# Second cross-attention of a two-layer decoder: three score rounds of four heads become two rounds of two heads

## The reference, cut to what matters

```
x = _layernorm(x + _L1_xattn_ref(ctx_1024, ctx_1024, x, Wv, Wk, Wq, Wo, bo))
```

## Time and profile before

| what | value |
|---|---|
| median of three runs | 2841.48 us |
| the profiled execution's own time | 2838.83 us |
| its span from first to last instruction | 2837.0 us |
| mean granted TensorE clock | 0.942 of full |
| windows of the fifth block (first to last exponential) | about 2003 to 2493 us |

### The profile page before, as it was taken

One profiled execution on the slowest core, in us unless ns is written; L12 is line 12 of the kernel. 1 busy time (PEld: TensorE's weight loads), 2 busy tenths in 40 slices (PEclk: granted clock), 3 DMA queues, 4 the chain that ended last, 5 costly groups with the idle time before them and its releaser, 6 DMA issues.

```text
span 2837.0 us, 37833 instructions
## 1 busy us (share of the span) xinstructions
PE 2598.1 (92%) x14306; PEld 1562.2 (55%) x14310; DVE 1468.7 (52%) x3205; ACT 1126.7 (40%) x1614; POOL 1035.0 (36%) x702
## 2 busy tenths in 40 slices
PE   5786999999999999996999999688999999889997
PEld 3343556555556555654565666455434444468886
DVE  3443555555555555554433333266777776355555
ACT  3544344444444444442121121133576666631111
POOL 4666366666765676562100000242121112010001
PEclk8996999999999999997899999898899999789998
DMA  2001100000000000003899999410000000000000
GB/s 103 9 9 34 36 12 16 29 19 12 27 18 19 12 12 25 12 1 125 347 389 381 365 384 385 169 32 22 15 17 17 21 17 9 13 14 23 23 23 32
DMA packets 60196, 229.01 MB, mean 81 GB/s; under 512 B 16536, under 2 KB 30512, under 8 KB 44144
## 3 DMA queue, kind: packets, MB, share of 16 engines
q1 hardware_dynamic: 54128, 209.01, 20.1%
q0 software_dynamic: 3584, 9.84, 1.2%
q10 hardware_dynamic: 2304, 7.75, 0.7%
HBM read 216.73 MB, written 9.70 MB: 80 GB/s over the span
## 4 chain that ended last, share of the span: by engine, by line
PE 75%; DVE 7%; ACT 7%; issue 4%; DMA 3%; POOL 3%; SPq 0%; POOLq 0%; ACTq 0%; DVEq 0%
PE PS L680 8%; PE PS L1475 7%; PE PS L2074 6%; PE PS L663 6%; PE PS L711 5%; PE PS L1493 4%; PE PS L721 4%; PE PS L2062 4%; ACT y_P L1192 4%; PE PS L1120 3%; PE PS L695 3%; DMA m_fb<-in_m_fb 3%; PE PS L1137 3%; PE PS L1103 2%; PE PS L744 2%
## 5 line engine op out<-in xcount | busy, mean ns | idle before, releaser
L944 POOL TENSOR_TENSOR x_A<-x_A,x_P 128x1024 f32<-128x1024 f32 x190 | 451.1, 2374 | 205.8 <-ACT x_P L791 191.8
L871 DVE CUSTOM_DVE_ANT_0 x_junk<-PS,x_mb 128x512 bf16<-128x512 f32 x512 | 331.0, 685 | 351.8 <-PE PS L695 351.6
L1243 DVE TENSOR_REDUCE y_Mx<-PS 128x1 f32<-128x512 f32 x512 | 326.2, 684 | 124.7 <-PE PS L1137 123.1
L791 ACT ACTIVATE x_P<-PS,x_kb 128x1024 f32<-128x1024 f32 x256 | 271.9, 1111 | 224.4 <-PE PS L667 222.3
L1192 ACT ACTIVATE y_P<-PS 128x1024 f32<-128x1024 f32 x256 | 248.4, 1024 | 128.7 <-PE PS L1120 127.1
L1475 PE MATMUL PS<-m_w,m_xt 128*128 128x512 f32 x624 | 283.2, 597 | 0.6 <-issue 0.6
L680 PE MATMUL PS<-x_P,x_V 128*64 128x512 f32 x1024 | 247.1, 604 | 0.0
L663 PE MATMUL PS<-x_Q,x_K 64*128 64x512 f32 x1536 | 229.8, 403 | 0.0
L2074 PE MATMUL PS<-n_xp,n_wp 128*128 128x512 f32 x816 | 211.4, 409 | 4.3 <-POOL n_wp L2190 4.3
L1696 POOL DMA_INDIRECT m_xb<-xd,m_idxi x39 | 37.0, 949 | 404.9 <-PE PS L1463 372.0
L1475 PEld LDWEIGHTS PS<-m_w,m_xt 128*128 128x128 f32 x624 | 116.5, 192 | 116.9 <-issue 115.0
(11 more groups left out here) (331 smaller groups left out, 4210.9 us busy)
## 6 DMA issues: line engine op xcount, KB each, us to landing
m_w<-in_m_w SPq DMA_DIRECT2D x39, 2048.0 KB, 11.5
m_fb<-in_m_fb SPq DMA_DIRECT2D x39, 1024.0 KB, 13.3
m_v<-in_m_w SPq DMA_DIRECT2D x39, 1024.0 KB
x_w<-in_x_w SPq DMA_DIRECT2D x32, 384.0 KB, 3.1
ys<-m_yb SPq DMA_DIRECT2D x39, 128.0 KB
n_wg<-in_n_w SPq DMA_DIRECT2D x17, 256.0 KB, 2.8
x_cT<-in_ctxT SPq DMA_DIRECT2D x4, 1024.0 KB, 5.8
y_c<-in_ctxT SPq DMA_DIRECT2D x6, 512.0 KB, 3.6
```

The costliest lines, as they stand in the source:

```text
L791: act.e.activation(Pt[gt % 6][:], PS[:, 2 * i:2 * i + 2, :], ACT.Exp, bias=kb[u // 8 % 2][:, kt:kt + 1], scale=scale).then_inc(s["exp"], 1)
L871: dve.e.tensor_tensor_reduce(junk[j % 2][:], ring.bank("max", v, j), mb[b % 2][:, half * 512:half * 512 + 512], 1.0, -3e38, ALU.add, ALU.m ...
L944: pool.e.tensor_tensor(A[u % 2][:], Pt[(gt - 1) % 6][:] if kt == 1 else A[u % 2][:], Pt[gt % 6][:], ALU.add).then_inc(s["add"], 1)
L1243: dve.e.tensor_reduce(Mx[v % 2][:, h, qt, half:half + 1], ring.bank("max", v, j), AX.X, ALU.max).then_inc(s["red"], 1)
```

## The change

- The scores are made in two halves of two heads: heads 0 and 1 ("sc", 0), then heads 2 and 3 ("sc", 1). Each half has two rounds instead of three: 8 matmuls for four heads instead of 12.
- The columns of the projection matrices are doubled, so that rows 16 to 31 of a band hold the keys and the queries a second time. The second key tile now holds the keys as they are in rows 0 to 15 and the low part in rows 16 to 31. The first round multiplies it with the doubled high part of the queries, 32 rows deep. The second round is high keys x low queries, with row 16 for the ones and the maxima, 17 rows deep.
- GpSimd makes the second key tile with two instructions (a product with the column `part`, then a subtraction) in place of one. ScalarE's high part of the keys is a copy without a bias.
- The ones of row 16 are written by one more DMA per group (4 partitions x 4 KB), ahead of the four rows of the maxima, which go to `Q[..][1]`.
- Each half waits only for the exponential that last read its two banks, and each exponential only for its half.
- The order of a window becomes: first half of the scores, two maxima (now of heads 2 and 3), the side work except pv and ev, second half, two maxima (heads 0 and 1), pv, ev, and what `after` lists. "turn" moves into `after`, "mq" behind the first two maxima.

```diff
             after = {0: [("st", -2, 0), ("xb", 0, 0)], 1: [("nr", -2, 0)], 2: [("tp", -2, 0)], 3: [("rec", -1, 0)], 4: [("tp", -2, 1)],
-                     5: [("mul", -1, 0)], 6: [("res", -1, 1)], 7: [("res", -1, 3)]}
-            at = {t: ([("mq", 1, 0)] if t == 5 else []) + maxima(t)[:2] + between[t] + maxima(t)[2:] + after[t] for t in range(T)}
+                     5: [("turn", 1, 0), ("mul", -1, 0)], 6: [("res", -1, 1)], 7: [("res", -1, 3)]}
+            at = {t: [("sc", 0, 0), *maxima(t)[:2], *([("mq", 1, 0)] if t == 5 else []), *[w for w in between[t] if w[0] not in ("pv", "ev")],
+                      ("sc", 0, 1), *maxima(t)[2:], *[w for w in between[t] if w[0] in ("pv", "ev")], *after[t]] for t in range(T)}
...
-                return j // 8, j // 4 % 2, j % 4
+                return j // 8, j // 4 % 2, (2, 3, 0, 1)[j % 4]
...
-            def scores(pe, gt):
+            def scores(pe, gt, half):
+
                 u, t = gt // T, gt % T
-                if not 0 <= u < n:
-                    return
                 Ku, Qu = K[u % NBK], Q[u % NBK]
-                if t == 0:
+                if t == 0 and half == 0:
                     pe.wait_ge(s["lo"], 3 * (u + 1))
-                    pe.wait_ge(s[f"row{u % 2}"], 16 * 4 * (u // 2 + 1))
-                for pp in range(2):
-                    pe.wait_ge(s["exp"], 2 * gt + pp - 1)
-                for i, (k, q, rows) in enumerate(((0, 0, 17), (0, 1, 16), (1, 0, 16))):
-                    for h in range(4):
+                    pe.wait_ge(s[f"row{u % 2}"], 16 * 5 * (u // 2 + 1))
+                pe.wait_ge(s["exp"], 2 * gt + half - 1)
+                for i, rows in ((1, 32), (0, 17)):
+                    for h in (2 * half, 2 * half + 1):
                         r = slice(32 * h, 32 * h + rows)
-                        m = pe.e.matmul(one_bank[h], Ku[k][r, t * P:(t + 1) * P], Qu[q][r, :], start=i == 0, stop=i == 2)
+                        m = pe.e.matmul(one_bank[h], Ku[i][r, t * P:(t + 1) * P], Qu[1 - i][r, :], start=i == 1, stop=i == 0)
                 m.then_inc(s["score"], 1)
...
-                            o, bias = (K[v % NBK][0][:, r], kone[:, 0:1]) if name == "k" else (Q[v % NBK][0][:], 0.0)
-                            act.e.activation(o, ring.bank(name, v, j), ACT.Identity, bias=bias).then_inc(s["hi"], 1)
+                            o = K[v % NBK][0][:, r] if name == "k" else Q[v % NBK][0][:]
+                            act.e.activation(o, ring.bank(name, v, j), ACT.Copy).then_inc(s["hi"], 1)
...
-                            pool.e.tensor_tensor(w[1][:, r], F[p % 3][:], w[0][:, r].bitcast(F32), ALU.subtract).then_inc(s["lo"], 1)
+                            if name == "k":
+                                pool.wait_ge(s["lo"], p)
+                                pool.e.tensor_scalar(M[:], K[v % NBK][0][:, r].bitcast(F32), part[:, 0:1], None, ALU.mult).then_inc(s["part"], 1)
+                                pool.wait_ge(s["part"], 2 * v + j + 1)
+                                pool.e.tensor_tensor(K[v % NBK][1][:, r], F[p % 3][:], M[:], ALU.subtract).then_inc(s["lo"], 1)
...
+                            sp.e.dma_start(K[v % NBK][0][16:P:32, :].bitcast(F32), ones[:]).then_inc(s[f"row{v % 2}"], 16)
                             for h in range(4):
-                                sp.e.dma_start(Q[v % NBK][0][32 * h + 16:32 * h + 17, :].bitcast(F32),
+                                sp.e.dma_start(Q[v % NBK][1][32 * h + 16:32 * h + 17, :].bitcast(F32),
                                                NM[v % 2][h:h + 1, :].bitcast(F32)).then_inc(s[f"row{v % 2}"], 16)
```

More of the change, by code:

```diff
@@ L992, in l1_cross @@
         def l1_cross(c, wy, nx):
-            wo, bo, wqk, wv, kone = wy["wo"], wy["bo"], wy["wqk"], wy["wv"], wy["kone"]
+            wo, bo, wqk, wv, part = wy["wo"], wy["bo"], wy["wqk"], wy["wv"], wy["part"]
             cT = [wy["c0"], wy["c1"]]
             n, T, NBK, scale = 16, 8, 3, 1.0 / 16
-            s = stage_sems(c, 4, "y", "proj hi cf lo vm vc one max red mq turn nm score exp pv ev rec mul ob res xb "
+            s = stage_sems(c, 4, "y", "proj hi cf lo vm vc one ones part max red mq turn nm score exp pv ev rec mul ob res xb "
                                       "row0 row1 den0 den1 dc0 dc1 dr0 dr1 rb0 rb1 gsq gpow gs gtp gT xsq xpow rt lg sig chain")
@@ L1028, in l1_cross @@
                 4: [("pv", 0, 4), ("v", 2, 1)],
-                5: [("pv", 0, 5), ("turn", 1, 0)],
+                5: [("pv", 0, 5)],
                 6: [("pv", 0, 6), ("wo", -1, 0), ("res", -1, 0), ("wo", -1, 1)],
@@ L2241, in program @@
         with ExitStack() as c1:
-            wy = {n: sbuf(c1, f"y_{n}", sh) for n, sh in (("wo", [P, 4, D]), ("bo", [P, D]), ("wqk", [P, 2, 2, P]), ("wv", [P, P]), ("kone", [P, 1]),
+            wy = {n: sbuf(c1, f"y_{n}", sh) for n, sh in (("wo", [P, 4, D]), ("bo", [P, D]), ("wqk", [P, 2, 2, P]), ("wv", [P, P]), ("part", [P, 1]),
                                                          ("c0", [P, SX]), ("c1", [P, SX]))}
```

46 lines of the change are left out of this document (27 added, 19 removed).

## The result

The first measurement of the changed kernel gave 2818.01 us as the median of four runs (2813.86 to 2822.52), beside 2839.5 for four runs of the kernel before: a ratio of 0.9936 [0.9915, 0.9957]. That is 15 us less than the forecast of 2833, inside the range, and a gain of 0.64%. It was not the whole story.

| measurement | changed | before beside it | ratio, 95% |
|---|---|---|---|
| first | 2818.01 (2813.86–2822.52, 4 runs) | 2839.5 (4) | 0.9936 [0.9915, 0.9957] |
| second | 2828.7 (2812.39–2849.63, 12) | 2835.2 (29) | 0.9985 [0.9965, 1.0005] |
| third | 2829.09 (2817.71–2849.43, 12) | 2838.39 (23) | 0.9977 [0.9956, 0.9998] |

A forecast was written before the change was run, and what follows sets the result against it. The prediction took the block to be bound by a hand-over between TensorE's scores and ScalarE's exponentials. Its terms summed to -5.7 us, from 2838.8 to 2833 us, with its own range 2822 to 2844 and a wide range 2800 to 2858.

The forecast's parts named there:

- the ring: Three banks for four maxima: the fourth waits for VectorE's first reduction; plain windows 3.05 us against 3.16.
- The five steps: Plain window from first score to next matmul: 0.34, 0.53, 0.75, 0.43 and 1.00 us, sum 3.05.
- The ring does not hold TensorE: Rival: fourth maximum finds its bank free, VectorE's reductions bound plain windows at about 2.5 us; 2803 us, chance 0.17.
- Window 5: Window where "turn" moves behind pv, its transposes now uncovered: +0.44 us, 14 times, +6.2 us.
- tp: Work in window 4 after a batch, now uncovered in `after`: 3 times +0.55 us, +1.7 us.
- wo: Windows with "wo" and the two behind: bounds 0 and -2 us per batch, -1 taken, -3 in all.
- Start: First windows at 1.2 GHz and a fifth DMA delaying first scores: bounds 0 and +6, +3.5 us taken.
- Tail: Last ten windows, mostly without maxima, ring empty: bounds -13 (clock stays up) and 0, -6 us taken.
- The rows of the maxima: DMA rows before a group's first scores: cover shrinks from about 3.5 to 2.1 us, costed at nothing.
- The rule weighed: One more tiling-mode change in some 45 projection windows: 0.2 us each would make the sum +3, not -6.
- the tail keeps its full clock and the loop is a little shorter: Rival: start and tail at their good ends, 0.05 us less per window; about 2818 us, chance 0.22.
- The slower rival: Maxima do not run beside the other pair's scores, costing 0.24 us per window or more; 2861 us, chance 0.12.

## Why the prediction was right or wrong

**The loop.** Right, and it decided the case: the hand-over went, the ring closed, and of 1.22 us of idle time 0.19 were gained. The five steps measured 0.81 (for 0.34 + 0.53), 0.75, 0.42 and 1.00; the sum was 2.98 and not 3.05. The step that was off is the first: the first maximum starts beside the first round (2192.22 and 2192.23), not behind the second, and its reduction starts 0.81 later all the same. Two edits that lengthen this one step, a third round (1.05 us) and maxima of the same heads (1.01 us), lengthen the plain window by as much, to 3.21 and 3.17 us: that is the loop shown by experiment. "The ring does not hold TensorE" was wrong: the fourth maximum waits 0.57 us for VectorE. Whether covering that wait with pv would pay is not shown; in pairs of windows at full clock it did not.

**The terms.** Measured outside group 0, which is counted as the start. k, k, q: -2.1 forecast, 10 x -0.43 = -4.3 measured. v: -1.8, measured 12 x -0.21 = -2.5. Plain: -4.2, measured -6.2 in 36 windows, nearly all of them -0.19. Window 5: +6.2, measured 0.22 to 0.34 in thirteen of them, +3.7, and -0.6 in that of group 14, where no maxima are left. "tp": +1.7, measured 3 x 0.40 = +1.2. Each was summed some 0.1 us per window too dear, about the size of the missed overlap. "wo": -3 forecast, -2.1 measured: -5.2 in the six "wo" windows and +3.2 in the three windows behind each batch. In the second and third batch a dip of the clock of 3.4 us lay in a "wo" window before and in a window of the next group after, so single windows there tell less than this sum. Start: +3.5, measured +2.4 in group 0 and +0.7 ahead of it. Tail: -6 halfway between -13 and 0, measured -11.1: the term that was mis-sized most. The clock was low for 10 of the 33.5 us, not all through; two of the windows took 1.9 us, the pace of ScalarE alone, the others 2.8 to 3.6 and the one with the router's matmuls 9.97 (13.8 before).

**The rows of the maxima.** Costed at nothing, with a cover of 2.1 us from the end of the DMA train to the group's first scores. It measured 2.18 (2199.49 to 2201.67). The sign of being wrong, first scores that wait for a DMA, came once all the same: ahead of group 8 they stood 0.4 us for these rows, and the window was 3.48 us long.

**The rule weighed.** I charged nothing for a change of tiling mode more per projection window. k, q and v windows measured 3.51 to 3.64 us, on or below the 3.65 of the ring. The Trainium skill, "TensorEngine Tiling (Array Packing)", Key Properties, says that a change of tiling mode drains TensorE. Had each such change cost the 0.2 us that the prediction weighed, the path of a "v" window (3.63 us) would have been 3.8; it measured 3.58. The trace shows 0.42 us from the last maximum to pv, a step that the sum had, and nothing beyond it.

**The sum.** -5.7 forecast. The profiled span is 22 us shorter, of which 7 lie ahead of the block and are no effect of the change; the block itself gives -15 with what lies around it. Over 28 runs the median gain is 9 us, near the forecast's 6, and over the first four it was 21. That 9 lies so near 6 is in part luck: where the clock held, the block gained more than twice the forecast, and falls of the clock, for which the forecast had no term beyond the start and the tail, took part of it back in other runs. The rival "the tail keeps its full clock and the loop is a little shorter" (2818; its terms add up to 2816) describes the first four runs and the profile; the forecast (2833) describes the other 24 better. Which of the two a run is depends on the clock, and that no step of mine had.

**What was missed.** The slower rival had a mechanism that is real (0.2 us per plain window when maxima and scores can't run together) but does not occur. The danger was elsewhere: four variants of order, heads or rounds came out slower by 102 to 311 us, most of it because TensorE stayed at or fell to 1.2 GHz. I read 0.52 in the earlier trace rows as a property of the tail; in the kernel before the clock was low in the first windows too (0.50 from 1973.8 to 2011.3), and whether it rises there is decided anew in each kernel. A rival "the clock rises one batch later", at some 100 us, belonged in the list with a chance of a few per cent.

**What stays open.** What raises or drops the clock here. The share of busy records doesn't tell it: 0.51 with 238.75 of 240 us busy in one kernel, 1.00 with 17.09 of 20 in another. In the kernels where it stayed low, it rose for good or for a while near the first batch of "wo" (2230 to 2248), long rows of full-array products; yet nine such products strewn in did not do it. That slower windows keep the clock low and the low clock keeps the windows slow is only argued. Open too is why the pairs of windows with pv first at full clock give back what they gain in the window behind them.

## What to carry to other kernels

When a wait between two engines is broken, list the buffers that are fewer than their users, and follow the in-order queue behind each of them: the next loop can be summed from rows of the kernel before, here to 0.07 us. A reordering of small tiled matmuls should be judged by two numbers, the loop at full clock and the stretches at which clock it ran, and by ten runs rather than four where the clock differs from run to run. If the clock falls in the windows right behind a dense part, some spare dense work there can hold it up and be worth more than it costs. And a shorter window is a gain only if the windows behind it are no longer than before: add up over all of them.

## What was not expected of the hardware

- A matmul that stands behind two rounds in the program started with the first of them (2192.23 beside 2192.22, the second round at 2192.56); it uses other row bands. With maxima in the same bands it starts 0.58 us behind the first score (2374.16 after 2373.58). The reduction that reads it starts 0.81 us after the first score in the one case and 1.01 in the other.
- Much the same work ran for 270 us at 1.2 GHz in one variant (halves with three rounds) and 37 us in another (the kernel before, low from 1973.8 to 2011.3), with TensorE busy for 97% of the first (220.58 of 227 us) and for 95% of the second (34.30 of its last 36 us).
- One kernel on the same data gave 2812 and 2850 us, with mean clocks of 0.949 and 0.933.
